# Wider score products for the row maxima in a fused attention and feed-forward kernel

## What is computed

```python
h = concat([tokenise(x), txt], axis=1)            # 16 x 192 x 64
h = h + plain_attention(layernorm(h))             # stage A
h = h + top_k_ffn(layernorm(h))                   # stage A
# stages B and C: 16 query heads, one key/value head, window of 128
q, k = rmsnorm(rope(x @ wq.T)), rmsnorm(rope(x @ wk.T))
mask = (cols <= rows) & (rows - cols <= 128)
scores = where(mask, einsum('bqgtd,bqgsd->bqgts', q, k) / 8, -1e30)
attn = softmax(scores, axis=-1)
h = h + einsum('bqgts,bqgsd->bqgtd', attn, v) @ wo.T
h = h + one_of_32_experts(layernorm(h))           # stage D
```

## Time and profile before

| | |
|---|---|
| median of three runs | 530.15 us (525.23 to 530.69) |
| time of the profiled execution | 525.05 us |
| its span, first to last instruction | 523.3 us |
| mean granted TensorE clock in the span | 0.951 of full speed |
| TensorE (PE) busy | 474.7 us, 91% |
| weight loads (PEld) busy | 375.0 us, 72% |
| VectorE (DVE) busy | 345.2 us, 66% |
| ScalarE (ACT) busy | 316.0 us, 60% |
| GpSimd (POOL) busy | 235.3 us, 45% |
| chain that ended last, by engine | PE 43%, DVE 31%, ACT 12%, POOL 7% |

### The profile page before, as it was taken

The page is one execution under the profiler, slowest core; times in us unless marked ns, Lnnn a source line. Parts: engine busy times, 40 slices in busy tenths (PEclk is TensorE's granted clock), DMA queues, the critical chain, the costliest instruction groups (busy, mean ns, idle before and its releaser), DMA issues.

```text
span 523.3 us, 14268 instructions
## 1 busy us (share of the span) xinstructions
PE 474.7 (91%) x5765; PEld 375.0 (72%) x5771; DVE 345.2 (66%) x1151; ACT 316.0 (60%) x675; POOL 235.3 (45%) x266
## 2 busy tenths in 40 slices
PE   8878889989998999989988999989998999789986
PEld 4434577777886888768866888877876887677764
DVE  3588679657985679567975589568956695235221
ACT  2337565776667666685667675677668556454322
POOL 3347633764357424752456514753465236520010
PEclk9999999998999789997999699999999799879999
DMA  8340240022101210042001210032003200231000
GB/s 301 96 95 1 48 95 1 2 48 64 22 11 41 53 32 4 2 88 56 3 4 41 63 30 4 3 82 50 10 3 74 50 2 2 43 70 28 4 1 9
DMA packets 13969, 21.38 MB, mean 41 GB/s; under 512 B 5024, under 2 KB 6544, under 8 KB 13776
## 3 DMA queue, kind: packets, MB, share of 16 engines
q1 hardware_dynamic: 13904, 20.47, 16.8%
HBM read 5.07 MB, written 0.79 MB: 11 GB/s over the span
## 4 chain that ended last, share of the span: by engine, by line
PE 43%; DVE 31%; ACT 12%; POOL 7%; issue 5%; DMA 1%; POOLq 0%; ACTq 0%; DVEq 0%
PE bank L1078 33%; PE bank L1109 10%; DVE negm L690 4%; DVE q_sb L625 4%; DVE tb L625 4%; DVE ssq L641 4%; DVE on L707 2%; POOL qs L874 2%; ACT qT L899 2%; POOL q_sb L867 1%; ACT qs L899 1%; ACT xf L910 1%; POOL rsA L801 1%; ACT kE L899 1%; DVE rec L703 1%
## 5 line engine op out<-in xcount | busy, mean ns | idle before, releaser
L832 POOL TENSOR_TENSOR q_sb<-q_sb,tb 128x1024 f32<-128x1024 f32 x24 | 57.2, 2382 | 99.1 <-DVE tb L625 99.1
L690 DVE TENSOR_REDUCE negm<-bank 128x2 f32<-128x384 f32 (+2 forms) x112 | 68.1, 608 | 47.0 <-PE bank L1078 46.4
L899 ACT ACTIVATE qT<-bank 128x512 fp32r<-128x512 f32 x96 | 52.6, 598 | 48.5 <-PE bank L1109 47.7
L1078 PE MATMUL bank<-kS,qM 128*128 128x128 f32 (+2 forms) x384 | 69.7, 302 | 7.1 <-issue 4.3
L1078 PEld LDWEIGHTS bank<-kS,qM 128*128 128x128 f32 x384 | 60.3, 211 | 21.9 <-issue 9.4
L874 POOL TENSOR_TENSOR qs<-q_sb,qs 128x1024 fp32r<-128x1024 f32 x24 | 56.6, 2359 | 27.9 <-ACT qs L899 27.8
L1078 PE MATMUL bank<-vx,p 128*64 128x65 f32 x1024 | 65.8, 224 | 0.0
L1031 ACT ACTIVATE p<-bank 128x512 f32<-128x512 f32 x96 | 54.9, 592 | 15.3 <-PE bank L1078 14.9
L1078 PEld LDWEIGHTS bank<-vx,p 128*64 128x64 f32 x1024 | 57.6, 138 | 0.0
L1078 PE MATMUL bank<-qT,kh 128*128 128x512 f32 (+1 forms) x128 | 55.4, 476 | 1.9 <-ACT p L1031 1.2
L1109 PE MATMUL bank<-ident_r,qs 128*128 128x128 f32 x384 | 48.3, 273 | 3.5 <-POOL qs L874 2.4
(11 more groups left out here) (177 smaller groups left out, 1036.0 us busy)
## 6 DMA issues: line engine op xcount, KB each, us to landing
qM<-qT SPq DMA_DIRECT2D x48, 256.0 KB, 3.2
qM<-qM SPq DMA_DIRECT2D x1, 1280.0 KB, 9.3
wts<-weights SPq DMA_DIRECT2D x1, 1059.0 KB, 6.4
p<-masks SPq DMA_DIRECT2D x1, 960.0 KB, 10.3
h<-txt SPq DMA_DIRECT2D x1, 672.0 KB, 7.5
img<-images SPq DMA_DIRECT2D x8, 72.0 KB, 2.4
q_sb<-wqkv SPq DMA_DIRECT2D x1, 576.0 KB, 8.5
p<-experts SPq DMA_DIRECT2D x1, 512.0 KB, 10.9
```

The lines of the kernel that those rows point to most:

```text
L690: ve.tensor_reduce(dst, src, AX_X, ALU.max, negate=True).then_inc(s_vec, 1)
L832: return gp.tensor_tensor(a, a, b[:, :, ::-1], ALU.add)
L899: return ac.activation(dst, src, ACT.Copy)
L1078: return pe.matmul(dst, lhsT, rhs, start=start, stop=stop, skip_group_check=True)
```

## The change

Each product of a unit may now stream more key columns than are needed: up to 224 (`S_WIDE`), but no further than the end of the bank (column 512) and no further than the end of the keys (`KEYS`, 384). The starts in the bank stay where they were. What a product writes beyond its own w columns is overwritten by the following products of the same unit, and the last product of a unit ends at the same column as before.

```diff
+S_WIDE = 224
...
+FILL = {}
...
+        ident_b = ident.bitcast(BF16)
...
+                    for _ in range(FILL.get((key[0], key[1], p.n), 0)):
+                        mm(bank[BANK_A][:, PT:512], ident_b[:, 0:P], ident_b[:, 0:P], True, True)
                     step(p)
...
                     for j, h in enumerate(heads[::2]):
                         q = qM[:, t, f, h:h + 2, :].rearrange("k h t -> k (h t)")
-                        ins = mm(bS[:, w * j:w * j + w], q, kS[u][:, b, lo:lo + w], True, True)
+                        at = w * j
+                        wide = min(max(w, S_WIDE), 512 - at, KEYS - lo)
+                        ins = mm(bS[:, at:at + wide], q, kS[u][:, b, lo:lo + wide], True, True)
```

## The result

The changed kernel takes 512.25 us (median of 4 runs, 511.42 to 514.33) against 529.68 us of the kernel before (4 runs, 525.23 to 530.69); the ratio is 0.969, with a 95% interval from 0.963 to 0.976. The forecast was 510 us, with a range of 503 to 521. The profiled execution took 511.42 us where the one before took 525.05, 13.6 us less.

What follows compares the result with a forecast made beforehand. TensorE was taken as the bound, busy 474.7 of 523.3 us, with 51.2 us at half clock. 525.05 - 16.4 for cleared slow clock + 1.0 for surplus columns = 509.7, so 510 us, range 503 to 521.

Steps and rivals of the forecast that it cites:

- The place: Falls come around S2, image products and a 128-column unit in pairs 1 to 6; the change adds streaming there.
- The cause: Many short products stream little though TensorE reads busy; 2304 columns in place of 1024 before a fall keep the clock up.
- What is left: Of 51.2 us at half clock, 3.4 us in the last pair and one 6.8 us stretch behind S2 stay.
- the other signs: In the profile after: mean clock near 0.98, whole pairs at 54 to 55 us, negm waiting no longer than before.
- The cost of the surplus: In S0 to S5, 25,088 extra columns cost +1 us, ends 0 and 10.5 us.
- The reasoning by the loads' pace: In S2, weight loads set 0.113 us from start to start, so 224 columns streaming for 0.093 us stay hidden.
- The price of slow clock: Over the pairs, each microsecond at half clock costs 0.4 us, ends 0.2 and 0.5; 41 us cleared give 16.4 us.
- the two readings: Price of slow clock from pairs compared: 0.38 over S0 to S6, 0.40 over whole pairs.
- The base: Sum starts from the profiled execution's 525.05 us, 5.1 us under the median 530.15; 510 us forecast as the median too.
- the clock does not follow width: Rival: busy share or step order counts, all eight slow stretches remain, 526 us up to 530; chance 0.12.
- The falls move: Rival: in half the pairs the fall comes later, among logits and transposes; some 20 us cleared, 518 us; chance 0.2.
- The surplus isn't hidden: Rival: in S0 to S5 the extra columns cost 10.5 us and the clock stays as is, 536 us; chance 0.06.

Runs made afterwards that it cites:

- the halves: The change with only S2 and S5 wide, 520.14 us, and with only S0, S1, S3, S4 wide, 523.21 us.
- the widths: The changed kernel with S_WIDE at 128, 256 or 384 in place of 224: 520.66, 512.41 and 514.12 us.
- the moved filler: Kernel before with narrow score products, plus three bfloat16 products of 128 columns on a constant in each of S6 to S13: 533.83 us.
- filled gaps: Changed kernel plus bfloat16 filler products ahead of the three places where its profile had clock falls: 514.94 us.
- the 37 runs: Runs of the unchanged kernel before, in three sets on three chips, each with its slow time: median 529.4 us.
- The filler: Kernel before with narrow score products, plus eight bfloat16 products of 128 columns in each S2 and S5, two in S0, S1, S3, S4: 524.73 us.

## Why the prediction was right, and where it was off

The mechanism held. **The place**: the time came out of the stretch from `S0` to `S6`, 13.66 us of 13.7. **The cause**: more streaming in that stretch keeps the clock at 2.4 GHz for longer; the halves, the widths and the moved filler show it. One reading behind it was not exact: in the pair of the earlier trace rows the unit of 128 columns starts at 292.61, 0.08 us before the fall, so it was hardly in the stretch ahead of it; in pairs 1, 2, 3 and 5 it was. **What is left**: I left 10.2 us of slow clock, with one fall in the last pair, and the profile has 10.2 us with one fall there; the other two were one stretch of 6.8 in my sum and came as two of 3.4, one of them outside the part that I had named. That it agrees to the tenth is luck, as the eight runs range from 7.1 to 24.8 us; their mean is 11.5. Of the other signs, the clock came out at 0.990 (0.98 forecast), five whole pairs at 54.0 to 55.7 us (54 to 55), and TensorE kept the maxima (`negm`) waiting for less: VectorE stood idle ahead of them for 39.3 us in place of 47.0.

**The cost of the surplus** was set at +1 us out of 0 to 10.5. No cost shows, by the line and by `S2`'s 1.08 us. The reasoning by the loads' pace (0.113 us against 0.093 for 224 columns) was right, and 384 columns show what a surplus past the cover costs. The 0.21 us from start to start at half clock was read with a duration that mixes both clocks (0.29 us); with the 0.38 us that a product lasts there it is 0.195, still over the 0.187 of 224 columns. That the cover holds at half clock as well shows in the profile with filled gaps, where `S5` falls wholly into the slow stretch from 450.36 to 457.19 and takes the 1.75 us of the narrow unit:

```profile
454.78 1.75 PE L1083 MATMUL bank<-kS,qM 128*128 128x224 f32 x8
```

**The price of slow clock** was the term that was mis-sized: 0.40 us per us, where the profiled pair of executions gives (525.05 - 511.42) / (51.2 - 10.2) = 0.33 and the 37 runs 0.319. Rounded clocks are not to blame: with the slow time of each pair taken from the stretches themselves the two readings give 0.38 and 0.43. They used pairs 1 to 5 only. Pair by pair, from `S0` to `S6`, the change took off 1.44, 3.11, 2.35, 3.66, 0.61, 0.80 and 1.69 us for 3.4, 8.6, 6.8, 10.2, 3.4, 3.4 and 6.8 us less slow clock. That is 0.34 to 0.42 in pairs 1 to 4, 0.18 to 0.25 in pairs 5 to 7, and 0.32 in sum: the price is not one number, and the readings had caught its upper part. 16.4 us were forecast for the cleared time and 13.6 came, which with the +1 that was not needed makes the difference from 510 to 511.4; the two errors partly cancel. The ends 0.2 and 0.5 held it.

**The base** rested on a guess, that the slower runs of before had more slow clock and that the change would take this too. The runs bear it out (529.3 at 61.2 us, 519.8 at 31.1; none of the change above 24.8), and so the medians are 17.4 us apart and not 13.6.

Of the rivals, *the clock does not follow width* is refuted by every width: the products start and end as before, and the slow time falls. *The falls move* is true in small: one fall at a new place in the profile, and others in the runs after it, with some 11 us left and not 31. *The surplus isn't hidden* is refuted for 224 columns, and but for 0.03 us per unit for 256.

The Trainium skill, page "TensorE: Matmul & The Clock Gate", section "Why this matters for your kernels", names pauses between bursts as what lowers the clock. The fall in the last pair agrees with it in kind (1.36 of 3.41 us busy before it), though its pause of 2.05 us is shorter than the gap that the page warns of; most falls that the change removed do not, since TensorE was shown as busy for 2.93 to 3.10 us of 3.41 before them.

What stays open: whether columns streamed is the exact measure, or something close to it. The filler, with nearly as many columns in the same units, left 26.6 us of slow time and the wide products 11.5; and width 128, with 896 surplus columns, did as well as `S2` and `S5` alone with 1984.

## What to carry to other kernels

Where TensorE's clock falls although its row says busy, look at how much the array streams there: here eight products of 64 columns, each with weights of its own, took the same 1.08 us as eight of up to 224. Widening them into space that a later product overwrites cost nothing that could be measured while streaming stayed shorter than the weight load, 3.3 us with 384 columns. Look for the place, too: filler in other units of the pair left most of the falls. Before judging such a change, record the granted clock of every run and set the times against it, since one profile shows one draw of the slow time.

## What was not expected of the hardware

The slow time of one and the same kernel varies between 31.1 and 78.8 us from run to run, and it alone explains the spread of its times: 519.8 to 534.2 us, with no run further than 1.2 us from a straight line. A microsecond at half clock cost 0.32 us, although TensorE was shown as busy for 50.2 of 51.2 us in the slow stretches; I had expected 0.4. Even units without a pause gained less than one half: `S3` 0.36 of 1.02 us, `S5` 0.78 of 1.75. And five falls came after 2.93 to 3.10 us of work in 3.41, so the share for which a row shows TensorE as busy does not tell where its clock will fall.
